# The routing chain cut into single VectorE steps between the maxima of round zero, and its scatters moved from round 0 to rounds 2, 4, 6 and 8

## The reference

```
xn  = layernorm(x)
q, k, v = split(xn @ w_attn + b_attn);  rotate q and k by head number    # 16 heads of 32
o   = softmax(causal(q k^T)) * 512**-0.5 @ v;  attention = o @ w_proj + b_proj
probs = softmax(xn @ gate_w^T);  topw, sel = top_k(probs, 2);  topw /= sum(topw)   # 8 experts
expert e: (silu(g) * u) @ w2[e],  g, u = split(xn @ w1[e]^T)             # width 352
experts(xn)[t] = sum over the two chosen e of topw * expert_e(xn[t])
```

## Time and profile before

| | |
|---|---|
| time, three runs | 883.91, 884.51, 885.0 us; median 884.51 |
| profiled execution | 886.54 us, span 884.8 us, granted clock 0.974 |
| PE busy | 812.0 us (92%) |
| DVE, ACT, POOL busy | 542.7 (61%), 400.9 (45%), 256.0 us (29%) |

### The profile page before, as it was taken

One profiled execution on the slowest core, in us unless ns is written; L12 is line 12 of the kernel. 1 busy time (PEld: TensorE's weight loads), 2 busy tenths in 40 slices (PEclk: granted clock), 3 DMA queues, 4 the chain that ended last, 5 costly groups with the idle time before them and its releaser, 6 DMA issues. The chain is left out here.

```text
span 884.8 us, 14115 instructions
## 1 busy us (share of the span) xinstructions
PE 812.0 (92%) x4115; PEld 575.6 (65%) x4116; DVE 542.7 (61%) x1369; ACT 400.9 (45%) x790; POOL 256.0 (29%) x314
## 2 busy tenths in 40 slices
PE   3789999789999999999999999989999999999990
PEld 3769989556555555555555556777777777777760
DVE  5993543386566566666657755666666666666640
ACT  3231221103555555565555631355566666666630
POOL 3683000043233324323333262002322222222220
PEclk9899999979999999999999999999999999999995
DMA  9476785995566655677762116834564664644436
GB/s 318 159 238 198 231 277 184 300 218 175 158 182 152 226 127 164 145 239 194 184 171 57 16 44 192 289 112 125 117 168 72 169 169 74 166 71 71 71 43 207
DMA packets 80480, 143.25 MB, mean 162 GB/s; under 512 B 16688, under 2 KB 30512, under 8 KB 80368
## 3 DMA queue, kind: packets, MB, share of 16 engines
q1 hardware_dynamic: 43200, 65.72, 24.1%
q10 hardware_dynamic: 29056, 58.28, 23.9%
q0 software_dynamic: 8176, 18.65, 10.8%
HBM read 81.21 MB, written 61.15 MB: 161 GB/s over the span
## 5 line engine op out<-in xcount | busy, mean ns | idle before, releaser
L1408 ACT ACTIVATE probs<-scores_t 128x512 f32<-128x512 f32 (+3 forms) x384 | 163.7, 493 | 138.4 <-PE scores_t L1558 121.3
L913 DVE TENSOR_TENSOR w_lo<-w,w_hi 128x704 fp32r<-128x704 f32 x156 | 131.6, 885 | 88.4 <-ACT w_hi L827 71.8
L1578 PE MATMUL o_acc<-probs,v_ones 128*64 128x512 f32 (+3 forms) x768 | 146.0, 502 | 0.0
L1535 PE MATMUL maxima<-k_stack,q_stack 96*128 96x512 f32 (+3 forms) x384 | 138.9, 370 | 7.2 <-DMA q_stack<-qk_hi 2.7
L1558 PE MATMUL scores_t<-q_stack,k_stack 98*128 98x512 f32 (+3 forms) x384 | 136.6, 381 | 4.7 <-DMA q_stack<-row_lo 2.3
L1442 DVE TENSOR_REDUCE mx<-maxima 128x1 f32<-128x512 f32 x128 | 88.3, 690 | 83.9 <-PE maxima L1535 82.3
L1438 DVE CUSTOM_DVE_ANT_0 masked_scores<-maxima,mask_m 128x128 f32<-128x128 f32 (+3 forms) x256 | 121.4, 486 | 22.0 <-PE maxima L1535 13.9
L976 PE MATMUL gu<-w_hi,rows_hi 128*128 128x352 f32 x312 | 119.4, 383 | 2.7 <-DVE w_lo L913 2.7
L827 ACT CAST w_hi<-w 128x704 fp32r x156 | 114.2, 784 | 9.3 <-issue 9.3
L1558 PEld LDWEIGHTS scores_t<-q_stack,k_stack 98*128 98x128 f32 x384 | 71.8, 189 | 67.0 <-issue 41.6
L994 PE MATMUL down<-w,hidden_t 128*128 (+1 forms) x234 | 108.2, 598 | 0.8 <-DVE hidden_t L896 0.8
(11 more groups left out here) (182 smaller groups left out, 1275.4 us busy)
## 6 DMA issues: line engine op xcount, KB each, us to landing
w<-in_w_t SPq DMA_DIRECT2D x8, 1408.0 KB, 6.6
routed<-blank_row ACTq DMA_DIRECT2D x20, 514.0 KB, 6.7
rows<-routed ACTq DMA_DIRECT2D x39, 256.0 KB, 4.6
qk_hi<-st_hi SPq DMA_DIRECT2D x32, 256.0 KB, 4.7
qk_lo<-st_lo SPq DMA_DIRECT2D x32, 256.0 KB, 6.2
q_stack<-qk_hi ACTq DMA_DIRECT2D x32, 256.0 KB, 4.5
k_stack<-qk_hi ACTq DMA_DIRECT2D x26, 256.0 KB, 5.5
v_all<-o_t SPq DMA_DIRECT2D x4, 1536.0 KB, 5.7
```

Source lines behind the costliest of these rows:

```text
L913: nc.vector.tensor_tensor(w1_lo[r][:, k, :], w1_rows(slot, k), as_f32(w1_hi[r][:, k, :]), ALU.subtract).then_inc(w1_done, 1)
L1408: nc.scalar.activation(probs[:, k % PR, h, 0:w], scores_t[e % RING][:, 0:w], ACT.Exp).then_inc(exp_done, 1)
L1535: nc.tensor.matmul(mb[at % RING][:, 0:w], q_st[i][0:3 * HD, h, t * P:(t + 1) * P], k_st[i][0:3 * HD, h, c * CH:c * CH + w], start=True, st ...
L1578: last = nc.tensor.matmul(o_acc[c][2 * HD * h:2 * HD * (h + 1), CH - w:CH], v_st[i][:, j, h:h + 2, :].rearrange("p o d -> p (o d)"), probs ...
```

## The change

The chain becomes a generator. Its first part clears the two `prefix` buffers and copies both counts out of the banks (the ranks into a new buffer `rank`); then the new semaphore `counts_read` goes up, and TensorE's first scores wait for that instead of `slots_done`. The rest is cut by `yield` into 21 pieces; `block.vector` takes one piece after each unit of round 0. POOL's eight scatters in round 0 go, with their waits; its wait for `slots_done` moves to round 1, step 4, ahead of four scatters; rounds 2, 4, 6 and 8 send seven each. So number 15 is now the fifth one of round 4, and the wait ahead of number 16 stands in round 4 instead of round 2.

```diff
@@ route: dve_part
+        dve.wait_ge(counted, 2)
         for b in prefix:
             link(V.memset(b[:, 0:NT // 2, :], 0.0))
+        link(V.tensor_copy(prefix[0][:, NT // 2:, :], total_ps[:, 0:NT * E].rearrange("p (a e) -> p a e", e=E)))
+        link(V.tensor_copy(rank[:], rank_ps[:, 0:NT * E].rearrange("p (a e) -> p a e", e=E)))
+        V.sem_inc(counts_read, 1)
+        yield
         dve.wait_ge(consts, 4)
-        dve.wait_ge(counted, 2)
-
-        link(V.tensor_copy(prefix[0][:, NT // 2:, :], total_ps[:, 0:NT * E].rearrange("p (a e) -> p a e", e=E)))
         at, step = 0, 1
         while step < NT:
             now, then = prefix[1 - at], prefix[at]
             link(V.tensor_tensor(now[:, NT // 2:, :], then[:, NT // 2:, :], then[:, NT // 2 - step:NT // 2 - step + NT, :], ALU.add))
+            yield
...
+        yield
+        link(V.tensor_tensor(place[:], rank[:], place[:], ALU.add))
...
+        yield
         V.tensor_copy(keep["slot"][:], slot_f[:]).then_inc(slots_done, 1)
@@ attend
-    SENT_FIRST = 8
     SENT_NEXT = 4
-    SENT_PER_ROUND = 5
+    SENT_PER_ROUND = 7
@@ block.gpsimd
-            pool.wait_ge(slots_done, 1)
...
-                    if n == 0 and k < SENT_FIRST:
-
-                        pool.wait_ge(exp_done, (k + 1) * PAIR)
-                        scatter(next(sent))
                     if k == TPC and n == 1:
+                        pool.wait_ge(slots_done, 1)
                         for number in itertools.islice(sent, SENT_NEXT):
                             scatter(number)
@@ block.vector
-            route_dve(dve)
+            steps_of_route = route_dve(dve)
+            next(steps_of_route)
             dve.wait_ge(consts, 4)
             for slot in range(-LEAD, 0):
                 ahead(slot)
             for n in range(ROUNDS):
                 for u in range(NU):
                     ahead(n * NU + u)
+                    if n == 0:
+                        next(steps_of_route, None)
@@ block.tensor
             pe.wait_ge(minus_ones, SETS)
-            pe.wait_ge(slots_done, 1)
+            pe.wait_ge(counts_read, 1)
```

More of the change, by code:

```diff
@@ L570, in route @@
     over = m.sbuf("over", [P, E, NT], F32)
+    rank = m.sbuf("rank", [P, NT, E], F32)
     tiles = m.sbuf("tiles", [P, E], F32)
@@ L582, in route @@
     chain, counted = m.sem("chain_r"), m.sem("counted")
+    counts_read = m.sem("counts_read")
     owner_chain = m.sem("owner_chain")
@@ L634, in dve_part @@
         for e in range(1, E):
+            yield
             link(V.tensor_tensor(upto[:, e:e + 1], upto[:, e - 1:e], tiles[:, e:e + 1], ALU.add))
+        yield
         link(V.tensor_tensor(base[:], upto[:], tiles[:], ALU.subtract))
+        yield
         link(V.scalar_tensor_tensor(place[:], base[:].unsqueeze(1).to_broadcast([P, NT, E]), float(P),
                                     before_tile, ALU.mult, ALU.add))
-        link(V.tensor_tensor(place[:], rank_ps[:, 0:NT * E].rearrange("p (a e) -> p a e", e=E), place[:], ALU.add))
+        yield
+        link(V.tensor_tensor(place[:], rank[:], place[:], ALU.add))
         for j in range(TOPK):
+            yield
             last = V.tensor_tensor(picked[:, j], mask[:, j], place[:], ALU.mult)
         link(last)
+        yield
         link(V.tensor_reduce(slot_f[:].rearrange("p j a -> p (j a)"), picked[:].rearrange("p j a e -> p (j a) e"), AX.X, ALU.add))
+        yield
         V.tensor_copy(keep["slot"][:], slot_f[:]).then_inc(slots_done, 1)
@@ L668, in dve_owners @@
         V.tensor_copy(keep["expert_end"][:], ends[:]).then_inc(owners_done, 1)
-    return pool_part, pe_part, dve_part, dve_owners, slots_done, owners_done
+    return pool_part, pe_part, dve_part, dve_owners, slots_done, owners_done, counts_read
 def experts(nc, keep, scratch, x, b_proj, w1_t, w2_t, out):
@@ L1173, in attend @@
         shares_flat = scratch["shares"].rearrange("s h t -> s (h t)").rearrange("s (p k) -> s p k", p=P)
-        route_pool, route_pe, route_dve, route_owners, slots_done, owners_done = route(nc, m, keep, scores_t[0:2])
+        route_pool, route_pe, route_dve, route_owners, slots_done, owners_done, counts_read = route(nc, m, keep, scores_t[0:2])
         block = ctx.enter_context(nc.Block())
```

## The result

| | before | after |
|---|---|---|
| time, four runs each | 883.45 to 885.0, median 884.21 us | 892.25, 895.25, 895.27, 899.58, median 895.26 us |
| ratio after / before | | 1.0113, 95% interval 1.0083 to 1.0144 |
| profiled execution | 886.54 us, span 884.8 | 892.25 us, span 890.5 |

The change makes the kernel slower by 1.1%, some 10 us (the medians lie 11.05 apart, the spans of the two profiled executions 5.7). The forecast of 886.2 and its range up to 890.4 missed that; the rival that seven are as bad as eight gave 894.6. The profiled execution is the fastest of its four.

The account below looks back on a forecast made before the run. TensorE was taken to bound what the change can move, before 400 us. Terms: -4.2 + 0.8 + 4.2 + 0.9 = +1.7, giving 888.2 us for the profiled execution, 886.2 on the median's scale; range 881.3 to 890.4.

Parts of the forecast that it names:

- the rival that seven are as bad as eight: Rounds 2, 6 and 8 each lose 4.2 us, clock's fall included: +10.1, so 894.6; chance 0.15.
- Chain out of the front, 0: Ahead of round 0: no gain, since the load of `q_stack` sets TensorE's first maximum at 188.04; bounds 0 and 0.2.
- a first maximum before 188: Sign of a wrong prediction: TensorE's first maximum was to start still at about 188.0.
- the bound of 0.2: Upper bound for taking the chain out of the front: the time by which the chain ends after the load.
- Pieces, +0.8: Round 0: 21 chain pieces between VectorE's units return banks late; 0.8 us taken, half of 1.6; bounds 0 and 5.7.
- Eight out of round 0, -4.2: Round 0: without eight scatters the late signals to VectorE and ScalarE go, gaining 4.2 us; bounds 0 and 4.2.
- Seven in rounds 2, 6 and 8, +4.2: Seven scatters instead of five return a bank late; TensorE stands 1.6, 0.9 and 1.6 us, 4.2 together.
- I take no fall: Rounds 2, 6 and 8: the clock was taken not to fall behind the 1.6 us standstill; the fall kept for the range.
- round 6's 0.43: Round 6: VectorE's late unit 0.43 behind the fifth scatter's end, giving standstill 0.9; the argument against seven as bad as eight.
- Round 4's wait, +0.9: Round 4: number 16's wait for sixteen landed scatters delays the mask of step 8, costing TensorE 0.9 us; bounds 0 and 2.2.
- Transfers, 0: Four rounds with two more scatters beside the row of maxima: taken 0, between 0 and 1.15 us each.

Follow-up runs that it names:

- experiment 1: Changed kernel with four scatters in each of rounds 1 to 8 instead of four and sevens, chain still in pieces; 892.37 us, ratio to before 1.0053.
- experiment 10: Changed kernel, chain in pieces, no more than five scatters in a row, eight sent behind the mask of step 11 in rounds 1, 2, 4, 5, 6; 883.16 us, ratio 0.9976.
- 6: Kernel before with its eight scatters of round 0 split into four at steps 0 to 3 and four at steps 8 to 11; 882.27 us, ratio 0.9969.
- experiment 2: Changed kernel with the chain run whole ahead of the first unit again, scatters as in the change; 893.24 us, ratio 1.0081.
- experiment 3: Changed kernel with the chain whole in front and four scatters in each of rounds 1 to 8; 890.32 us, ratio 1.0045.
- 9: Changed kernel, chain whole in front, no more than five scatters in a row, eight sent behind the mask of step 11 in rounds 1, 2, 4, 5, 6; 883.61 us, ratio 0.9987.
- experiment 11: Kernel before with four of round 0's eight scatters moved behind the mask of step 11: one in round 1, two in 2, one in 6; 885.08 us, ratio 0.9996.
- 4: Changed kernel with two scatters (numbers 16 and 17) moved from round 4 to round 5; 894.38 us, ratio 1.0104.
- 7: Changed kernel with each scatter writing 512 bytes a row instead of 2056 into its own buffer, experts on blank rows; 894.31 us, one run.
- 8: Changed kernel with six scatters in a row in rounds 2, 4 and 8, seven in round 6, three left over behind the mask of step 11; 898.22 us, one run.
- 12: Changed kernel with each scatter made a plain transfer of the same rows from POOL's queue, experts on blank rows; 897.8 us, one run.
- 5: Changed kernel with its sevens sent as five at step 4 and two behind the mask of step 11; 887.87 us, ratio 1.0025.

## Why the prediction was wrong, point by point

- **Chain out of the front, 0:** right that the load sets the first maximum, and that VectorE is not late for it: it begins that unit some 0.45 us behind in all fourteen kernels, with the chain in front or without. Its sign of being wrong, a first maximum before 188, came (187.53) and says nothing of the chain: with the chain in front it comes at 186.3 to 188.0 too. But the front did not stay as it was. From the first maximum to the first turn it takes 13.6 to 13.8 us in the six kernels with the chain in front and in experiment 1, and 12.3 in the seven others with pieces. In the former the clock falls to 0.50 behind the load's wait, in the latter it stays at 1.00. That is 1.2 us gained, more than the bound of 0.2. What decides it no run shows: the length of the wait does not (2.84 without the fall in experiment 10, 2.19 with it in 6), and experiment 1 has the pieces and the fall.
- **Pieces, +0.8:** right. From the first turn of the units to the turn in round 1 it takes 39.08 to 39.12 us with pieces and no scatters in round 0, 38.13 to 38.19 with the chain in front: 0.95. Counted from the first maximum it is 51.4 with pieces (52.7 in experiment 1) and 51.7 to 51.8 with the chain in front (2, 3, 9 and 11), since the gain of 1.2 in the front goes against the 0.95. The tensor_scalar and the cast went down to 0.16 and 0.33, since POOL had nothing beside them; the Trainium skill's rule on shared ports (SBUF — State Buffer, Who interferes with whom) agrees.
- **Eight out of round 0, -4.2:** right in cause, a little large: 41.92 before against 38.13 to 38.19, so -3.8. Splitting the eight brings most of it (20.4 in round 0), leaving four all of it (19.6).
- **Seven in rounds 2, 6 and 8, +4.2:** the step that failed. The place and the mechanism were right, and seven does what eight did; the size was not. The step was to carry over to the seventh scatter how long a signal stays away behind the fifth, 1.15 and in round 6 0.43. After the change VectorE took up the held unit 1.61, 1.65 and 1.89 us behind the end of the seventh. So the standstills were 1.87 to 2.20 in nine of nine places (after, 2 and 4), not 1.6, 0.9 and 1.6; and "I take no fall" was wrong in four of the nine. Without a fall such a round takes 21.6 to 21.8, 2.1 to 2.3 over 19.5 (five places: after's rounds 2 and 6, 2's round 8, 4's rounds 6 and 8); with one 23.1 to 24.3 (after's round 8, 2's rounds 2 and 6, 4's round 2, where the mean of 8 us around the standstill is 0.74 to 0.85). The mean of the nine is 22.5, so three rounds cost 9.0. (With the three places of 7 and round 6 of 8 it is thirteen standstills of 1.84 to 2.20, eight of them with a fall.) The reason given against the fall, round 6's 0.43, came from a run of five; behind five such a unit came 0.4 or 1.1 behind the end of the last in one round or another, and with seven round 6 is no better than the rest.
- **Round 4's wait, +0.9:** right place, too small and not steady: TensorE stood 1.97 and the clock fell, 3.6 us in all; 0.26 in experiment 2. The sixteen took 5.65, not the 4.57 taken over from round 2, which is the 1.1 by which the wait was longer; in experiment 2 they took 3.96.
- **Transfers, 0:** nearly right for the change (0.95 at the head of round 4, where 0.71 was before), wrong for other places, as experiments 1, 3 and 12 show.

With the measured sizes the terms of the prediction give -3.8 + 0.95 + 9.0, and 0.4 to 3.6 for round 4: +6.6 to +9.8; with the 1.2 gained in the front +5.4 to +8.6. The two profiled executions differ by 5.7: 1.7 less up to the first turn, 2.8 less from there to the turn in round 1, 2.0, 3.4, 2.1 and 3.7 more in rounds 2, 4, 6 and 8, and 1.0 less in all the rest. That is half of the 11.05 between the medians, since the change's profiled execution is its fastest, 3.0 below its median, and that of before lies 2.3 above its own. Which standstills bring the clock down differs between executions of the same code, and the three slower ones have a lower granted clock (0.967 to 0.972 against 0.975), which fits a spread of 892.25 to 899.58; that falls are the other half is not shown.

## What to carry to other kernels

Two scatters more in a row moved no more bytes in all and did not make POOL's masks late in rounds 2, 6 and 8, and yet cost 3 us a round: look for what the other engines hear late behind a run that exists already, and don't extrapolate its cost from the longest run that was still free. The place in the run counts as well as its length: a shift of 0.3 us made a run of four hold a signal for 2.3 us. A standstill near one that brought the clock down is to be priced with the fall. When work is moved to a quieter place, list what else is sent there: four scatters in round 3 or 7 were dearer than seven in an even round.

## What the runs showed of the hardware

Away from scatters VectorE starts 0.3 to 0.6 us behind the start of the matmul that it waits for, in nearly all places. While indirect transfers from POOL follow each other at 1.27 us, this lag depends on where in the run the matmul starts:

- 0.1 behind the start of a fourth: 0.43 to 0.49, but for 1.12 once (experiment 3);
- 0.5 to 1.0 behind a fourth: 0.9 to 1.4 (after and most others), and 2.4 and 2.95 in experiment 11 behind a unit that was late itself;
- 1.0 behind a third with a fourth to come: 2.3 to 2.4 (experiments 1, 3 and 11);
- 0.1 to 0.2 behind a fifth: 1.2 to 2.0 wherever VectorE stood idle for it (before, after, 2 and 4 to 11), but 0.43 behind the fifth of the eight in round 0 before;
- 0.1 to 0.2 behind a seventh: 2.4 to 2.8 (after, 2, 4, 7 and 8); 0.2 behind the eighth of round 0: 2.63.

Behind runs of one or two none was late where VectorE stood idle for it. ScalarE was held together with VectorE behind the seventh and the eighth (260.21 and 260.24 after). A quarter of the bytes left the standstills as they were (7), and seven plain transfers in 3.76 us held nothing (12). What in the chip holds the signals no run here shows.

A standstill of TensorE brought its clock from 1.00 to 0.50 in some executions and not in others: behind seven scatters, 1.84 to 2.20 us long, in eight of thirteen places; it fell behind a wait of 1.03 in experiment 11 as well, and not behind the 1.15 of the earlier trace rows.
